# Cross-attention kernel: two more probability tiles turned off TensorE, PSUM shared by halves, normalization on ScalarE

## The chip, the cores and the metric

One core of one Trainium2 chip. The metric is the device time of one execution in microseconds, median of several runs. Before the change it is 120.97 us (three runs: 120.93, 120.97, 122.6).

## What is computed

The reference, cut to the arithmetic; x is (2, 512, 512), the memory (2, 1024, 256), all float32:

```python
memory_proj = jnp.einsum('bme,de->bmd', memory, W_mem)
scores = jnp.einsum('bnd,bmd->bnm', hidden_states, memory_proj) / jnp.sqrt(jnp.float32(D))
attn = jax.nn.softmax(scores, axis=-1)
memory_context = jnp.einsum('bnm,bmd->bnd', attn, memory_proj)
gate_input = jnp.concatenate([hidden_states, memory_context], axis=-1)
gate = jax.nn.sigmoid(jnp.einsum('bnf,df->bnd', gate_input, W_gate) + b_gate)
fused = hidden_states + gate * memory_context
return _rmsnorm(fused, norm_w)
```

## The kernel before

The kernel never forms the projected memory. It projects the queries through W_mem (`queries`), multiplies them with the memory's first form, `ctxT` (`scores`), takes a softmax, multiplies the probabilities with the memory's second form, `ctxN` (`attended`), and uses W_mem and the gate weights behind that (`gate_weights`, `gate_from_x`, `gate_from_attended`, `context`). There are two batches of four tiles of 128 rows: tiles j = 0 to 3 and j = 4 to 7.

Each float32 operand is split in a high and a low part, and each product is three matmuls: high-high, high-low, low-high. ScalarE makes the high part of a loaded block (`split_hi`, L344), VectorE the low part by subtraction (`split_lo`, L472), GpSimd for blocks from 28 on (L318). Loads go by SyncE in the order of `blocks` into a ring of 10 slots; load i waits until block i - 10 is split both ways. So the order of `blocks` is the order in which operands come.

A tile's way through softmax: `scores(j)` on TensorE into a pair of PSUM banks, `row_max` on VectorE (L482), `exponentials` on ScalarE (L358), `normalize` on VectorE (L489) in `probs`, which has three slots. Then `attended` needs the probabilities with memory positions on the partitions. Tiles 0 to 3 are turned by TensorE against an identity (`turn`, 8 transposes a tile, L730) into a PSUM pair, and split from there (L371 high, L512 low). Tiles 4 to 7 are turned without TensorE: VectorE transposes 32x32 blocks (`square_up`, L500) into ring slots, SyncE writes them to DRAM (`send`, L267, 512 KB) and reads them back in another block order (`fetch`, L278, 4 DMAs of 128 KB), and ScalarE and VectorE split them (`placed_hi` L366, `placed_lo` L506). `attended(b)` waits for all four tiles of its batch: the high parts at its start, the low parts before the last third.

PSUM holds `wide`, three pairs of banks, and `acc`, one pair. A list `uses` gives each use of a pair of `wide` the pair of its place modulo 3; a use waits for the release of the use three before it. A `gate` use takes a whole pair: one bank for the gate's sums, one for `context`.

The order on each engine is written out by hand, and every engine executes in order. `banks`, `wait_banks`, the `blocks` list, the SyncE program and the written-out orders are what the change touches.

Of the kernel before, what the change touches and what calls it, by code (L numbers as in the profile page):

```python
# [5 lines left out]
def xattn_kernel(nc, xT, ctxT, ctxN, w_mem, w_memT, w_gateT, x_rows, b_gate, norm_w, out):  # L6
    f32 = mybir.dt.float32
# [5 lines left out]
    P = 128  # L13
# [15 lines left out]
    with ctx:  # L29
# [24 lines left out]


        QUAD = 32
        NQ = P // QUAD
        squares_of = [ring[:, 2 * n:2 * n + 2].rearrange("p a n -> p (a n)") for n in range(2)]
        placed = [ring[:, 2 * n:2 * n + 2].rearrange("p a n -> p (a n)") for n in range(2, 4)]
        passage = [nc.dram_tensor(f"passage{t}", [P, M], f32).ap() for t in range(T)]  # L60
# [5 lines left out]
        bias = sb("bias", [P, D])  # L66
        gain = sb("gain", [P, D])
# [4 lines left out]
        res = sb("res", [P, 2, D])  # L72
        neg_max = sb("neg_max", [P, B * T])
# [57 lines left out]
        for k in range(KD):  # L131
            wgT_block(k)
# [37 lines left out]
        landed = [sem(f"landed{n}") for n in range(2)]  # L170
        q_hi, q_lo = sem("q_hi"), sem("q_lo")
# [16 lines left out]
        def nth_chunk(b, c):  # L188
# [3 lines left out]
        uses = [("scores", 0), ("scores", 1), ("scores", 2), ("turn", 0), ("scores", 3), ("turn", 1),  # L192
                ("turn", 2), ("wc", 0), ("turn", 3)]
        uses += [("scores", 4), ("scores", 5), ("scores", 6), ("gate", 0), ("scores", 7)]
        uses += [("gate", j) for j in range(1, B * T)]

        def banks(kind, j):
            return uses.index((kind, j)) % PAIRS

        def wait_banks(eng, kind, j):  # L200
            n = uses.index((kind, j)) - PAIRS
            if n < 0:
                return
            kind, i = uses[n]
            if kind == "scores":
                eng.wait_ge(exped, i + 1)
            elif kind == "turn":
                eng.wait_ge(pT_lo, i + 1)
            elif kind == "wc":
                eng.wait_ge(wc_lo, KE)  # L210
            else:
                eng.wait_ge(gated, i + 1)
# [22 lines left out]
        def from_quarters(t):  # L235
            return placed[t % 2].rearrange("p (q k n) -> p q k n", q=NQ, k=KM)
# [4 lines left out]
        def _(sp):  # L241
            def load_x(j):
                sp.dma_start(xr[:, j % 2], x_rows[j]).then_inc(x_loaded[j % 2], 16)

            for i, (src, _, _, key) in enumerate(blocks):
                if i in BY_ACT:
                    continue
                if i >= RING:
                    wait_hi(sp, i - RING)
                    wait_lo(sp, i - RING)  # L250
                sp.dma_start(slot(i), src).then_inc(loaded[i], 16)
                if key == ("ctxT", 1, KE - 1, 1):
                    sp.dma_start(bias[:], b_gate.partition_broadcast(P)).then_inc(vec_loaded, 16)
                    sp.dma_start(gain[:], norm_w.partition_broadcast(P)).then_inc(vec_loaded, 16)
                    load_x(0)
                    load_x(1)
# [8 lines left out]
            def send(t):  # L265
                sp.wait_ge(squared_up, t + 1)
                sp.dma_start(passage[t], squares_of[t % 2]).then_inc(sent[t % 2], 16)  # L267

            def fetch(t):

                if t < 2:
                    wait_lo(sp, NB - 1)
                else:
                    sp.wait_ge(pT_lo, T + t - 1)
                sp.wait_ge(sent[t % 2], 16 * (t // 2 + 1))
                quarters = passage[t].rearrange("(q j) (r f) -> r j q f", q=NQ, r=NQ)
                for r in range(NQ):
                    sp.dma_start(placed[t % 2][r * QUAD:(r + 1) * QUAD].rearrange("j (q f) -> j q f", q=NQ),  # L278
                                 quarters[r]).then_inc(landed[t % 2], 16)

            send(0)
            fetch(0)
            send(1)
            fetch(1)
            send(2)
            next_x(2)
            fetch(2)
            store(0)
            send(3)
            fetch(3)  # L290
            next_x(3)
            store(1)
# [40 lines left out]
        def _(act):  # L333
# [18 lines left out]
            def exponentials(j):  # L352
                act.wait_ge(maxed, j + 1)
                if j - PROBS >= T:
                    act.wait_ge(squared_up, j - PROBS - T + 1)
                elif j >= PROBS:
                    act.wait_ge(turned, j - PROBS + 1)
                nc.scalar.activation(probs[:, j % PROBS].rearrange("p (h m) -> p h m", h=2),  # L358
                                     wide[:, banks("scores", j)], ACT.Exp, bias=neg_max[:, j:j + 1],
                                     accum_out=row_sum[:, j:j + 1]).then_inc(exped, 1)  # L360

            def placed_hi(t):
                act.wait_ge(landed[t % 2], 16 * NQ * (t // 2 + 1))
                if t == 0:
                    act.wait_ge(a_sum, nth_chunk(0, KE - 1))
                nc.scalar.activation(by_quarter(pT_s[0], t), from_quarters(t), ACT.Copy).then_inc(pT_hi, 1)  # L366

            def turned_hi(j):
                act.wait_ge(turned, j + 1)
                rows = slice(j % T * P, (j % T + 1) * P)  # L370
                nc.scalar.activation(pT_s[0][:, :, rows],  # L371
                                     wide[:, banks("turn", j)].rearrange("p h (k n) -> p (h k) n", n=P),
                                     ACT.Copy).then_inc(pT_hi, 1)

            def weight_hi(c):
                act.wait_ge(wc_sum, c + 1)
                nc.scalar.activation(wcT_s[0][:, c], wide[:, banks("wc", 0), c], ACT.Copy).then_inc(wc_hi, 1)
# [12 lines left out]
            def mean_square(j):  # L390
                act.wait_ge(fused, j + 1)
                if j == 0:
                    act.wait_ge(eps_set, 1)
                nc.scalar.activation(squares[:], gate[:, j % 2], ACT.Square, scale=SCALE,  # L394
# [6 lines left out]
            split_hi(11, 12, 13)  # L401
            exponentials(0)
            split_hi(14, 15)
            exponentials(1)
            split_hi(16)
            exponentials(2)
            turned_hi(0)
            split_hi(17, 18)
            turned_hi(1)
            exponentials(3)  # L410
            query_hi(1, 0)
            split_hi(19)
            query_hi(1, 1)
            turned_hi(2)
            split_hi(20, 21)
            weight_hi(0)
            turned_hi(3)
            split_hi(22, 23)
            weight_hi(1)
            split_hi(*range(24, 34))  # L420
# [3 lines left out]
            exponentials(4)  # L424
            exponentials(5)
            exponentials(6)
            gate_tanh(0)
            placed_hi(0)
            mean_square(0)
            exponentials(7)  # L430
            placed_hi(1)
            gate_tanh(1)
            placed_hi(2)
            mean_square(1)
            gate_tanh(2)
            placed_hi(3)
            mean_square(2)
            gate_tanh(3)
# [23 lines left out]
        def _(dve):  # L462
# [17 lines left out]
            def row_max(j):  # L480
                dve.wait_ge(scores_sum, j + 1)
                nc.vector.reduce_max(neg_max[:, j:j + 1], wide[:, banks("scores", j)], AXIS.XY,  # L482
                                     negate=True).then_inc(maxed, 1)
# [405 lines left out]
```

## Time and profile before

| | |
|---|---|
| median of three runs | 120.97 us |
| the profiled execution | 120.74 us |
| its span | 119.0 us |
| mean granted TensorE clock | 0.987 of full |
| ScalarE busy | 55.1 us (46%) |
| VectorE busy | 76.7 us (64%) |
| GpSimd busy | 19.5 us (16%) |
| the chain that ended last | 85% of the span on TensorE |

The span is the stretch of the execution in which instructions run; the rest of its 120.74 us, 1.7 us, lies around it. The page lists each engine's busy time, the span in 40 slices, the chain followed back from the last instruction, and the costliest groups of instructions. The timeline gives an instruction's start, its duration and, in brackets, how long its engine was idle ahead of it and what ended that. Matmuls overlap, so a matmul's duration is longer than the step from one start to the next.

### The profile page before, as it was taken

The page shows a single profiled execution, that of the slowest core. Times are in us where ns is not written, and L with a number is a line of the kernel's source. Part 1 is how long each engine was busy: PE and PEld are TensorE (multiplying, and loading weights), DVE is VectorE, ACT ScalarE, POOL GpSimd, SP SyncE. Part 2 cuts the span into 40 slices and gives each one's busy share as a digit, 9 for nine tenths or more (in the row PEclk, how much of TensorE's full clock was granted, in tenths as well). Part 3 has the DMA queues.
Part 4 walks back from the last instruction along what each step waited for, and adds up shares of the span by engine and source line. Part 5 has one row for each costly group of instructions (what it writes and reads, how often), then busy time and mean ns, then how long its engine had stood idle before and what let it go on. Part 6 is the DMA issues. An engine that isn't in the chain of part 4 may idle for free.

```text
span 119.0 us, 1570 instructions
## 1 busy us (share of the span) xinstructions
PE 112.3 (94%) x547; PEld 94.2 (79%) x547; DVE 76.7 (64%) x116; ACT 55.1 (46%) x100; POOL 19.5 (16%) x25
## 2 busy tenths in 40 slices
PE   6999999999999999999999999999999999999910
PEld 6878888888888888888888888888888888889900
DVE  0389969987999700459999857464662031777791
ACT  4498675559967930941624532512421030334511
POOL 2000000000000499692000300030301000011120
PEclk9999999999999999999999999999999999999995
DMA  3999992436955870000436495749222200044222
GB/s 54 338 343 357 390 389 77 150 111 187 265 198 167 248 258 10 0 0 0 176 116 237 116 323 158 293 116 241 83 88 102 80 0 0 0 123 141 88 88 88
DMA packets 11095, 18.45 MB, mean 155 GB/s; under 512 B 1232, under 2 KB 4048, under 8 KB 11088
## 3 DMA queue, kind: packets, MB, share of 16 engines
q1 hardware_dynamic: 10656, 17.70, 45.2%
q10 hardware_dynamic: 432, 0.66, 1.8%
q8 instruction: 4, 0.07, 0.2%
q14 instruction: 3, 0.02, 0.1%
HBM read 14.16 MB, written 4.19 MB: 154 GB/s over the span
## 4 chain that ended last, share of the span: by engine, by line
PE 85%; issue 4%; DVE 4%; ACT 2%; POOL 1%; POOLq 1%; DVEq 0%; ACTq 0%
PE wide L716 18%; PE acc L767 18%; PE wide L785 16%; PE acc L691 10%; PE wide L813 6%; PE wide L798 6%; PE wide L744 5%; PE wide L676 3%; PE wide L730 3%; ACT squares L394 2%; DVE gate L546 2%; DVE gate L539 2%; POOL rstd L323 1%; POOLq L29 1%; ACT res L457 0%
## 5 line engine op out<-in xcount | busy, mean ns | idle before, releaser
L323 POOL TENSOR_TENSOR rstd<-mean_sq,neg_half 128x1 f32<-128x1 f32 x8 | 5.9, 734 | 55.7 <-ACT squares L394 52.6
L358 ACT ACTIVATE probs<-wide,neg_max 128x1024 f32<-128x1024 f32 x8 | 8.9, 1116 | 8.4 <-DVE neg_max L482 8.4
L716 PE MATMUL wide<-ctxT_hi,qT_hi 128*128 128x512 f32 x32 | 12.6, 392 | 0.0
L716 PE MATMUL wide<-ctxT_hi,qT_lo 128*128 128x512 f32 x32 | 12.5, 389 | 0.0
L716 PE MATMUL wide<-ctxT_lo,qT_hi 128*128 128x512 f32 x32 | 12.5, 389 | 0.0
L318 POOL TENSOR_TENSOR wgT_lo<-ring,wgT_hi 128x512 fp32r<-128x512 f32 x4 | 5.4, 1373 | 38.9 <-ACT wgT_hi L344 38.9
L523 DVE TENSOR_TENSOR wgT_lo<-acc,wgT_hi 128x512 fp32r<-128x512 f32 x4 | 2.6, 686 | 13.6 <-ACT wgT_hi L383 13.6
L482 DVE TENSOR_REDUCE neg_max<-wide 128x1 f32<-128x1024 f32 x8 | 9.7, 1215 | 2.2 <-PE wide L716 2.1
L387 ACT ACTIVATE gate<-gate 128x512 f32<-128x512 f32 x7 | 4.4, 629 | 13.2 <-DVE gate L533 13.2
L785 PE MATMUL wide<-wgT_hi,xT_lo 128*128 128x512 f32 (+1 forms) x36 | 8.8, 365 | 0.0
L785 PE MATMUL wide<-wgT_lo,xT_hi 128*128 128x512 f32 (+1 forms) x36 | 8.8, 365 | 0.0
L785 PE MATMUL wide<-wgT_hi,xT_hi 128*128 128x512 f32 (+1 forms) x36 | 8.8, 365 | 0.0
L366 ACT ACTIVATE pT_hi<-ring 128x1024 fp32r<-128x1024 f32 x4 | 4.2, 1062 | 9.1 <-DMA ring<-passage 9.1
L506 DVE TENSOR_TENSOR pT_lo<-ring,pT_hi 128x1024 fp32r<-128x1024 f32 x4 | 4.9, 1222 | 5.0 <-ACT pT_hi L366 5.0
L394 ACT ACTIVATE squares<-gate 128x513 f32<-128x513 f32 x7 | 4.4, 628 | 7.5 <-DVE gate L546 7.5
L554 DVE SCALAR_TENSOR_TENSOR res<-gate,rstd,gain 128x512 f32<-128x512 f32 x7 | 5.2, 745 | 3.9 <-POOL rstd L323 3.9
L767 PE MATMUL acc<-pT_lo,ctxN_hi 128*128 128x512 f32 x32 | 7.6, 389 | 0.0
L767 PE MATMUL acc<-pT_hi,ctxN_hi 128*128 128x512 f32 x32 | 7.6, 389 | 0.0
L767 PE MATMUL acc<-pT_hi,ctxN_lo 128*128 128x512 f32 x32 | 7.6, 389 | 0.0
L383 ACT ACTIVATE wgT_hi<-acc 128x512 fp32r<-128x512 f32 x4 | 2.2, 596 | 11.7 <-PE acc L767 11.7
L785 PEld LDWEIGHTS wide<-wgT_hi,xT_hi 128*128 128x128 f32 x36 | 6.4, 188 | 1.2
L785 PEld LDWEIGHTS wide<-wgT_hi,xT_lo 128*128 128x128 f32 x36 | 6.4, 189 | 1.1
(91 smaller groups left out, 250.9 us busy)
## 6 DMA issues: line engine op xcount, KB each, us to landing
ring<-ctxT SPq DMA_DIRECT2D x8, 256.0 KB, 4.1
ring<-w_gateT SPq DMA_DIRECT2D x8, 256.0 KB, 5.5
ring<-ctxN SPq DMA_DIRECT2D x8, 256.0 KB, 5.4
xr<-x_rows SPq DMA_DIRECT2D x8, 256.0 KB, 3.3
passage<-ring SPq DMA_DIRECT2D x4, 512.0 KB, 3.6
ring<-passage SPq DMA_DIRECT2D x16, 128.0 KB, 2.8
out<-res SPq DMA_DIRECT2D x7, 256.0 KB, 2.0
ring<-xT SPq DMA_DIRECT2D x6, 256.0 KB, 5.5
```

The lines of the kernel that those rows point to most:

```text
L318: nc.gpsimd.tensor_tensor(lo, slot(i), hi.bitcast(f32), ALU.subtract).then_inc(lo_pool, 1)
L323: nc.gpsimd.tensor_tensor(rstd[:, col], mean_sq[:, col], neg_half[:], ALU.pow)\
L358: nc.scalar.activation(probs[:, j % PROBS].rearrange("p (h m) -> p h m", h=2), wide[:, banks("scores", j)], ACT.Exp, bias=neg_max[:, j:j + 1],
L394: nc.scalar.activation(squares[:], gate[:, j % 2], ACT.Square, scale=SCALE, accum_out=mean_sq[:, j:j + 1]).then_inc(squared, 1)
L482: nc.vector.reduce_max(neg_max[:, j:j + 1], wide[:, banks("scores", j)], AXIS.XY, negate=True).then_inc(maxed, 1)
L691: last = nc.tensor.matmul(acc[:, c], wm_s[left][:, c, k], xT_s[right][:, b, k], start=(k == 0 and (left, right) == (HI, HI)), stop=(k == K ...
L716: last = nc.tensor.matmul(wide[:, banks("scores", j), h], qT_s[left][:, c, rows], ctxT_s[right][:, c, cols], start=(c == 0 and (left, righ ...
L744: last = nc.tensor.matmul(wide[:, banks("wc", 0), c], wm_s[left][:, c, k], wgT_s[right][:, KD + k], start=(k == 0 and (left, right) == (HI ...
L767: last = nc.tensor.matmul(acc[:, c], ctxN_s[left][:, k, c * P:(c + 1) * P], pT_s[right][:, k], start=(k == 0 and (left, right) == (HI, HI) ...
L785: nc.tensor.matmul(wide[:, banks("gate", j), h, cols], xT_s[left][:, b, k, rows], wgT_s[right][:, k, cols], start=(k == 0 and (left, right ...
L798: last = nc.tensor.matmul(wide[:, banks("gate", j), h, cols], aT_s[left][:, c, rows], wcT_s[right][:, c, cols], start=False, stop=(left == ...
L813: last = nc.tensor.matmul(sums, aT_s[left][:, c, rows], wmT_s[right][:, c, cols], start=(c == 0 and (left, right) == (HI, HI)), stop=(left ...
```

## The change

1. Tiles 0 and 1 no longer go through `turn`. They take the way of tiles 4 to 7: block transpose on VectorE, `send`, `fetch`, split. Their squares lie in a new buffer `spare` and in `res`, their placed form in `xr` and in `vecs` (which holds bias and gain). The loads of x rows, bias and gain therefore wait for the low splits of tiles 0 and 1.
2. `normalize` moves from VectorE to ScalarE, as a copy with a scale; VectorE keeps the reciprocal (`invert`).
3. `uses` now names its pair and halves itself. Gate and context sums are uses of their own, of one half each; a gate half is free once `gate_arg` has read it.
4. The four blocks of gate weights for x (blocks 28 to 31 before) come as blocks 20 to 23, ahead of `ctxN` (now 24 to 27) and `ctxT` of the second batch (now 28 to 31, so that GpSimd makes its low halves).
5. The orders change. TensorE runs `scores(3)` ahead of the second batch's queries, `gate_from_x(0)` and `(1)` ahead of `attended(0)`, and spreads `context` behind later tiles.

```diff
+        EARLY = 2
+        BY_DMA = (*range(EARLY), *range(T, B * T))
+        squares_of = {0: spare[:], 1: res[:].rearrange("p a n -> p (a n)")}
+        placed = {0: xr[:].rearrange("p a n -> p (a n)"), 1: vecs[:].rearrange("p a n -> p (a n)")}
...
         for k in range(KD, 2 * KD):
             wgT_block(k)
+        for k in range(KD):
+            wgT_block(k)
         for j in range(KM // 2):
             ctxN_block(0, j)
...
-        for k in range(KD):
-            wgT_block(k)
...
+        BOTH = (0, 1)
+        uses = [("scores", 0, 0, BOTH), ("scores", 1, 1, BOTH), ("scores", 2, 2, BOTH), ("scores", 3, 0, BOTH),
...
+                ("context", 2, 0, (0,)), ("context", 3, 0, (1,)), ("gate", 5, 2, (1,)), ("gate", 6, 1, (0,)),
...
+            n = use_of[kind, j]
+            for half in uses[n][3]:
+                before = [u for u in uses[:n] if u[2] == uses[n][2] and half in u[3]]
+                if not before:
+                    continue
+                of, i = before[-1][0:2]
...
+                elif of == "gate":
+                    eng.wait_ge(arg_done, i + 1)
+                else:
+                    eng.wait_ge(gated, i + 1)
...
+            load(*range(27))
             send(0)
+            load(27, 28)
             fetch(0)
             send(1)
+            load(29, 30, 31, 32)
             fetch(1)
+            load(33, 34, 35, 36)
+            load_x(0)
+            load_x(1)
+            load_vecs()
+            load(37)
+            send(T)
+            send(T + 1)
+            fetch(T)
+            fetch(T + 1)
+            send(T + 2)
+            send(T + 3)
             next_x(2)
...
+            def normalize(j):
+                act.wait_ge(inv_done, j + 1)
+                nc.scalar.activation(probs[:, j % PROBS], probs[:, j % PROBS], ACT.Copy,
+                                     scale=inv_sum[:, j:j + 1]).then_inc(normed, 1)
...
-            def normalize(j):
+            def invert(j):
                 dve.wait_ge(exped, j + 1)
                 nc.vector.reciprocal(inv_sum[:, j:j + 1], row_sum[:, j:j + 1]).then_inc(inv_done, 1)
-                dve.wait_ge(inv_done, j + 1)
-                nc.vector.tensor_scalar(probs[:, j % PROBS], probs[:, j % PROBS], inv_sum[:, j:j + 1], None,
-                                        ALU.mult).then_inc(normed, 1)
...
+                if b == 0:
+                    pe.wait_ge(early_hi, EARLY)
+                pe.wait_ge(pT_hi, nth_tile(b, T - 1) - EARLY)
```

TensorE between the third turned tile and `attended(0)`, in the kernel before (L730 is `turn`, L744 `gate_weights`, L767 `attended`):

```order
L730 MATMUL wide<-ident,probs 128x128 x8
L744 MATMUL wide<-wgT_hi,wm_hi 128x512 x4
L744 MATMUL wide<-wgT_lo,wm_hi 128x512 x4
L744 MATMUL wide<-wgT_hi,wm_lo 128x512 x4
L767 MATMUL acc<-pT_hi,ctxN_hi 128x512 x16
```

and in the changed one (L809 is `turn`, L823 `gate_weights`, L868 `gate_from_x`, L850 `attended`):

```order
L809 MATMUL wide<-ident,probs 128x128 x8
L823 MATMUL wide<-wgT_hi,wm_hi 128x512 x4
L823 MATMUL wide<-wgT_lo,wm_hi 128x512 x4
L823 MATMUL wide<-wgT_hi,wm_lo 128x512 x4
L868 MATMUL wide<-wgT_hi,xT_hi 128x512 x4
L868 MATMUL wide<-wgT_lo,xT_hi 128x512 x4
L868 MATMUL wide<-wgT_hi,xT_lo 128x512 x4
L868 MATMUL wide<-wgT_hi,xT_hi 128x512 x4
L868 MATMUL wide<-wgT_lo,xT_hi 128x512 x4
L868 MATMUL wide<-wgT_hi,xT_lo 128x512 x4
L850 MATMUL acc<-pT_hi,ctxN_hi 128x512 x16
```

The last turn before `attended(0)` and its gate weights are as they were; 24 matmuls of `gate_from_x` now follow them.

ScalarE from the last splits of the second batch's queries input to the second batch's `query_hi`, before (L344 `split_hi`, L358 `exponentials`, L371 the high split of a turned tile, L350 `query_hi`):

```order
L358 ACTIVATE probs,row_sum<-wide,neg_max 128x1024
L344 ACTIVATE xT_hi<-ring 128x512 x2
L358 ACTIVATE probs,row_sum<-wide,neg_max 128x1024
L344 ACTIVATE wgT_hi<-ring 128x512
L358 ACTIVATE probs,row_sum<-wide,neg_max 128x1024
L371 ACTIVATE pT_hi<-wide 128x8x128
```

and after (L400 `split_hi`, L414 `exponentials`, L420 `normalize`):

```order
L400 ACTIVATE wgT_hi<-ring 128x512
L414 ACTIVATE probs,row_sum<-wide,neg_max 128x1024
L400 ACTIVATE wgT_hi<-ring 128x512 x2
L420 ACTIVATE probs<-probs,inv_sum 128x1024
L400 ACTIVATE wgT_hi<-ring 128x512 x2
L414 ACTIVATE probs,row_sum<-wide,neg_max 128x1024
L400 ACTIVATE wgT_hi<-ring 128x512
L420 ACTIVATE probs<-probs,inv_sum 128x1024
L414 ACTIVATE probs,row_sum<-wide,neg_max 128x1024
L400 ACTIVATE wgT_hi<-ring 128x512
L420 ACTIVATE probs<-probs,inv_sum 128x1024
```

Three normalizations stand between the exponentials, and the splits ahead of the first exponential have grown by three.

SyncE after the gate weights' loads, in the changed kernel (L282 loads, L305 `send`, L322 `fetch`; `ring` is the target of the loads, `spare` and `res` the squares of tiles 0 and 1, `xr` and `vecs` their placed form):

```order
L282 DMA ring<-ctxN 128x512 x3
L305 DMA passage<-spare 128x1024
L282 DMA ring<-ctxN 128x512
L282 DMA ring<-ctxT 128x512
L322 DMA xr<-passage 32x4x256 x4
L305 DMA passage<-res 128x1024
L282 DMA ring<-ctxT 128x512 x3
L282 DMA ring<-w_memT 128x512
L322 DMA vecs<-passage 32x4x256 x4
```

Before, this stretch held loads only; now two sends and two fetches of four DMAs each stand in the same queue, with loads behind each of their waits.

## Rows read from the trace of the kernel before

**Rows 1.** The page, parts 1 and 2: TensorE's busy time and its granted clock

```profile
PE 112.3 (94%) x547; PEld 94.2 (79%) x547; DVE 76.7 (64%) x116; ACT 55.1 (46%) x100; POOL 19.5 (16%) x25
...
PEclk9999999999999999999999999999999999999995
```

**Rows 2.** Waits: engine, line <- whom: total us, times, longest; then a weight load

```profile
PE wide L676 <- DVE warm L463: 1.0, 1, 1.0
...
PEld wide L744 <- DVE wgT_lo L472: 0.2, 1, 0.2
```

**Rows 3.** The chain that ended last, in order of time: start us, us, what

```profile
19.69 2.73 PE acc L691 x12
22.42 0.87 PE wide L730 x8
23.29 2.77 PE wide L716 x12
...
26.93 2.74 PE acc L691 x12
...
30.55 2.84 PE wide L744 x12
...
34.26 2.74 PE wide L744 x12
37.00 10.88 PE acc L767 x48
...
85.95 10.88 PE acc L767 x48
```

**Rows 4.** ScalarE's timeline: start us, us, line, operation, out<-in, idle before

```profile
15.55 1.12 ACT L358 ACTIVATE probs<-wide,neg_max 128x1024 f32<-128x1024 f32 x1 [1.82 <-DVE neg_max L482]
...
16.65 1.14 ACT L344 ACTIVATE xT_hi<-ring 128x512 fp32r<-128x512 f32 x2
...
37.53 2.18 ACT L344 ACTIVATE ctxT_hi<-ring 128x512 fp32r<-128x512 f32 x4
...
64.17 1.06 ACT L366 ACTIVATE pT_hi<-ring 128x1024 fp32r<-128x1024 f32 x1 [1.58 <-DMA ring<-passage]
...
82.84 1.07 ACT L366 ACTIVATE pT_hi<-ring 128x1024 fp32r<-128x1024 f32 x1 [2.34 <-DMA ring<-passage]
...
116.10 0.51 ACT L457 ACTIVATE res<-res,rstd 128x256 f32<-128x256 f32 x1 [1.55 <-POOL rstd L323]
```

**Rows 5.** VectorE's timeline, same columns

```profile
18.34 0.75 DVE L489 TENSOR_SCALAR probs<-probs,inv_sum 128x1024 f32<-128x1024 f32 x1
...
38.30 2.48 DVE L472 TENSOR_TENSOR ctxT_lo<-ring,ctxT_hi 128x512 fp32r<-128x512 f32 x4
...
50.63 1.23 DVE L482 TENSOR_REDUCE neg_max<-wide 128x1 f32<-128x1024 f32 x1 [1.03 <-PE wide L716]
...
56.01 1.23 DVE L500 STREAM_TRANSPOSE ring<-probs 128x1024 f32<-128x1024 f32 x1
```

**Rows 6.** SyncE's timeline, its DMA issues: a send and two fetches

```profile
57.27 0.33 SPq L267 DMA_DIRECT2D passage<-ring  x1
59.94 1.75 SPq L278 DMA_DIRECT2D ring<-passage  x4
...
77.47 1.74 SPq L278 DMA_DIRECT2D ring<-passage  x4
```

**Rows 7.** The page, DMA issues: count, KB each, us from issue to landing

```profile
ring<-w_gateT SPq DMA_DIRECT2D x8, 256.0 KB, 5.5
...
xr<-x_rows SPq DMA_DIRECT2D x8, 256.0 KB, 3.3
passage<-ring SPq DMA_DIRECT2D x4, 512.0 KB, 3.6
```

**Rows 8.** GpSimd's timeline: four splits

```profile
40.31 5.38 POOL L318 TENSOR_TENSOR wgT_lo<-ring,wgT_hi 128x512 fp32r<-128x512 f32 x4 [38.93 <-ACT wgT_hi L344]
```

**Rows 9.** Line 730, the turns' matmuls: ns min/median/max, first and last start

```profile
L730 PE MATMUL wide<-ident,probs x32: 270/272/273, 22.3 to 34.0; 128*128 128x128 f32 x32
```

More of the change, by code:

```diff
@@ L65, in xattn_kernel @@
         table = sb("table", [P, 1])
-        bias = sb("bias", [P, D])
-        gain = sb("gain", [P, D])
+        vecs = sb("vecs", [P, 2, D])
+        bias, gain = vecs[:, 0], vecs[:, 1]
+        spare = sb("spare", [P, M])
         xr = sb("xr", [P, 2, D])
@@ L241, in _, with load, load_vecs @@
         def _(sp):
+            def load(*ids):
+                for i in ids:
+                    if i in BY_ACT:
+                        continue
+                    if i >= RING:
+                        wait_hi(sp, i - RING)
+                        wait_lo(sp, i - RING)
+                    sp.dma_start(slot(i), blocks[i][0]).then_inc(loaded[i], 16)
             def load_x(j):
+                if j < 2:
+                    sp.wait_ge(early_lo, 1)
                 sp.dma_start(xr[:, j % 2], x_rows[j]).then_inc(x_loaded[j % 2], 16)
[L245 to L256, printed above, removed]
+            def load_vecs():
+                sp.wait_ge(early_lo, EARLY)
+                sp.dma_start(bias, b_gate.partition_broadcast(P)).then_inc(vec_loaded, 16)
+                sp.dma_start(gain, norm_w.partition_broadcast(P)).then_inc(vec_loaded, 16)
             def next_x(j):
@@ L715, in scores @@
                                     pe.wait_ge(q_lo, nth_chunk(b, c))
-                            last = nc.tensor.matmul(wide[:, banks("scores", j), h], qT_s[left][:, c, rows],
+                            last = nc.tensor.matmul(sums("scores", j, h), qT_s[left][:, c, rows],
                                                     ctxT_s[right][:, c, cols],
@@ L797, in gate_from_attended @@
                         for c in range(KE):
-                            last = nc.tensor.matmul(wide[:, banks("gate", j), h, cols], aT_s[left][:, c, rows],
+                            last = nc.tensor.matmul(sums("gate", j, h)[:, cols], aT_s[left][:, c, rows],
                                                     wcT_s[right][:, c, cols], start=False,
@@ L812, in context @@
                                 wait_lo(pe, index_of["wmT", c])
-                            last = nc.tensor.matmul(sums, aT_s[left][:, c, rows],
+                            last = nc.tensor.matmul(made, aT_s[left][:, c, rows],
                                                     wmT_s[right][:, c, cols],
@@ L825, in _ @@
                 queries(0, c, range(KD // 2, KD))
-            scores(0)
-            scores(1)
-            scores(2)
-            queries(1, 0, range(KD))
-            turn(0)
-            scores(3)
-            turn(1)
-            queries(1, 1, range(KD))
+            for j in range(T):
+                scores(j)
+            for c in range(KE):
+                queries(1, c, range(KD))
             turn(2)
@@ L837, in _ @@
             gate_weights(1)
+            gate_from_x(0)
+            gate_from_x(1)
             attended(0)
@@ L840, in _ @@
             scores(5)
-            for t in range(T):
-                if t < 2:
-                    scores(6 + t)
-                gate_from_x(t)
-                gate_from_attended(t)
-                context(t)
-            gate_from_x(T)
-            gate_from_x(T + 1)
+            gate_from_attended(0)
+            scores(6)
+            gate_from_attended(1)
+            scores(7)
+            context(0)
+            context(1)
+            for j in (2, 3):
+                gate_from_x(j)
+                gate_from_attended(j)
+            gate_from_x(4)
+            context(2)
+            context(3)
+            gate_from_x(5)
             attended(1)
-            gate_from_x(T + 2)
+            gate_from_x(6)
             for j in range(T, LAST):
```

301 lines of the change are left out of this document (169 added, 132 removed).

## The prediction

> **What bounds the kernel now.** I read the page first. TensorE (PE) is busy 94% of the span at nearly full granted clock [rows 1]. Busy time alone proves little for a pipelined engine, so I went to the waits: PE waited once, 1.0 us for its warm-up operand, and its weight loads once for 0.2 us in the gate-weight product [rows 2]. The chain that ended last says the same: from the first matmul to the last tiles it is one PE piece after another, with no issue time between them [rows 3]. So PE's instruction stream is the kernel, and the rest need only be in time. What PE no longer does is gained whole, unless something new is late. A step of 12 matmuls takes 10.88 / 4 = 2.72 us [rows 3]; all PE times below are chain times.
>
> **What leaves PE.** turn(0) and turn(1), 8 transposes each. From 22.42 to the end of the piece at 26.93 + 2.74 = 29.67 lie both turns and two 12-matmul steps: 7.25 - 2 x 2.72 = 1.81 us for two turns, with the slower restart behind each (2.77 and 2.74 instead of 2.72) [rows 3]. The first gate-weight product took 2.84 where the second took 2.74 [rows 3]: that is PE's 0.2 us wait for a low half of the gate weights [rows 2], of which 0.10 shows in the chain. In the new order DVE has split these halves by 26.1, well ahead of the product at 28.7, so 0.10 goes too. No matmul is added. Sum on PE: -1.91 us.
>
> **What is new on the others, and whether it is in time.** Durations: a split on ScalarE (ACT) advances it 0.52 us, (2.18 for four, less 0.1 of overlap with the next), an exponential with its accumulator read 1.10 (15.55 to 16.65), a 1024-column copy 1.06, or 0.97 after overlap [rows 4]. On VectorE (DVE) a row maximum is 1.23, a 32x32-block transpose 1.23, a split 0.60, and the normalization that goes away 0.75 [rows 5]. Normalizing on ACT is not in the trace. Lower bound: the 0.75 of DVE; upper bound: four times the 256-column scaled copy of the last tile, 4 x 0.51 = 2.04 [rows 4, 5]. I take 1.06, since the 1024-column copy is the same engine, size and function.
>
> PE now runs scores 0 to 3 from 11.53 to 22.41, the second batch's queries to 27.85, turn(2) to 28.7, gate weights, turn(3) at 31.46, gate weights, two gate_from_x from 35.07, attended(0) from 40.51 (before: 37.00).
>
> First batch on ACT: splits 14 to 16 fit ahead of the first exponential, which still starts at 15.55 behind row maximum 0. Then 2 splits, normalize(0) 17.7 to 18.8, 2 splits, exponential 1 from 19.7, a split, normalize(1) 21.8 (held by DVE's reciprocal behind its transpose), exponential 2 from 22.8, a split, normalize(2) 24.4 to 25.5, queries, exponential 3 from 25.9, normalize(3) 28.4 to 29.4. PE asks for tile 2 at 27.85 (2.3 us spare), tile 3 at 31.46 (2.0 spare), and the pair of scores(0) at 19.69, free since 16.75. At 2.04 each, three normalizations put tile 2 at 28.5 and four put tile 3 at about 33.4: PE would wait some 0.6, then 1.3 more; the change then gives nothing but 0.0 to 0.1 us. The cover is those 2 us.
>
> First transport, tiles 0 and 1: DVE turns blocks of tile 0 in 19.4 to 20.6 and of tile 1 in 24.4 to 25.6. Load 26 on SyncE (SP) needs the low half of block 16, made at 19.4, so it is out by 19.9 and the send goes at 20.7. Behind its wait stand loads 27 and 28, whose ring slots come free only at 22.5 and 24.3 anyway. A send takes 3.6 us [rows 7], and the first fetch row followed its send by 2.67 [rows 6]; so fetch(0) at 24.7 to 26.5, send(1) 26.5, loads 29 to 32 until 29.3, fetch(1) at 30.2. From a fetch's first issue to the high copy took 64.17 - 59.94 = 4.2 us in the best case and 82.84 - 77.47 = 5.4 in the worst [rows 4, 6]. So tile 1 lands at 34.4 to 35.6; ACT reaches it at 35.7, behind the second gate-weight copy, and is done at 36.8. PE wants it at 40.51: 3.7 us spare. The low half (DVE, by 38.1) is wanted two thirds through attended(0), at 47.8. The memory's second form (loads 24 to 27) is split by 37.2; GpSimd now makes the low half of the next batch's first form, at 1.35 us each from 37.8 on [rows 8], done by 43.2 and wanted at 51.4. So what hides the two tiles is the 5.44 us of gate_from_x put ahead of attended(0): without it tile 1 would be 1.7 us late.
>
> Second batch: row maximum 4 ends 1.4 us after scores(4), at 55.5, exponential 4 at 56.7; scores(6), which takes over its pair, starts at 58.2, 1.5 spare. Scores(7) wants exponential 5 (59.3) at 62.3. Of the shared halves the nearest is context(3), at 79.9 behind gate_arg(3), which DVE finishes at 77.7. The last tile's transport: blocks turned by 70.3 (before 69.2), send at once, fetch(7) behind fetch(6) and an x load at 76.2 instead of 77.47 [rows 6]; with the 5.4 us of the same tile before, the copy ends at 82.7. Attended(1) starts at 85.95 - 1.91 = 84.04 [rows 3], 1.3 spare, against 85.95 - 83.91 = 2.0 before [rows 3, 4]. The tail behind attended(1) has the same work and moves as a whole.
>
> **A rule against the row.** Rows first: the profile gives a transpose 272 ns [rows 9], while 8 of them take 0.87 us of the chain [rows 3], 109 ns each, since they overlap. The Trainium skill ("TensorE: Matmul & The Clock Gate", Part 4) has about 275 ns for a transpose in a kernel's context, "It's the only path that does a full 128×128 transpose in one shot". By it two turns would cost 16 x 0.275 = 4.4 us, an estimate. The trace agrees with the duration but not with the cost.
>
> [...]
>
> **Sum.** The profiled execution took 120.74 us, of which the span is 119.0. 120.74 - 1.91 = 118.83, span 117.1. The shown median, 120.97, is 0.23 above it, so as a median 118.8 to 119.1: I say 119.0, which is 1.6% less. A change within 2%, 118.55 to 123.4, is about what a measurement of this kernel can tell from none.
>
> **Rivals.** (A, forecast) PE stays gapless: 118.3 to 119.6. Chance 0.76.
>
> (B) Partly given back. Either ACT's normalizations are near 2.04 (up to 1.9 us of PE waiting, worked out above), or tile 7 is late by more than its 1.3 us at attended(1). For it: ACT and DVE now wait on each other in turn (reciprocal, normalize, block transpose), and SP's in-order queue passes each delay on. Against: a delay of 3.2 us is needed before everything is lost. 119.6 to 121.1, chance 0.11.
>
> (C) Slower: the first transport under load. Its transfers run beside the block loads. A 256 KB load took 5.5 us where the queue was full, 3.3 where it was not [rows 7]: a factor of 1.67. Then send(0) lands at 26.7, fetch(0) ends at 28.5, send(1) lands at 34.5, and fetch(1), at 5.4 x 1.67 = 9.0, at 43.5. The copy ends at 44.6, PE waits 4.1 us in front of attended(0), and the time is 122.9. It decides from 3.7 us of delay, and passes the old time from 5.6. Against it: the loads then queued are one by one, gated by ring slots, not a burst. Chance 0.08, of which 0.05 over 123.4 with knock-on delays.
>
> (D) Faster by far: the turns cost what their durations say, 16 x 0.272 = 4.35 us [rows 9], and the time is 120.97 - 4.45 = 116.5. Against it, the 0.87 us pieces. Chance 0.03. The remaining 0.02 I give to a gain that I don't see.
>
> **How the numbers follow.** Faster by over 2%: D, the unseen gain, and the lowest part of A (below 118.55, about 0.05): 0.10. Slower: 0.05. Within 2%: 0.85. The range for 8 in 10 starts at A's low end, 118.3, and takes in the upper bound of the normalization, 121.1. A's own range is 118.3 to 119.6.
>
> **What would show it.** Right: 16 transposes instead of 32; PE's waits still only the warm-up; attended(0) starting near 40.4 and attended(1) near 84.0; a span near 117.1. ACT's scaled copy near 1.06 us; turn(2) preceded by no idle time. Wrong: a PE wait for the copy out of vecs (C), for a turn's normalized tile, or for the copy out of the ring at attended(1) (B); or a span under 116.5 without waits (D). If normalize takes over 1.7 us, my ACT schedule fails; if the two fetches take over 9 us in all from send(1), my transport does.

## The result and the profile after

The changed kernel takes 119.06 us (median of six runs, 118.69 to 119.44) against 120.97 us before. The ratio is 0.985, 95% interval 0.983 to 0.988: 1.5% faster, and short of the 2% that count as more than no change. The profiled execution took 119.02 us with a span of 117.3. The ratios leave slow executions out, and the profiled ones of four versions below (normalization back on VectorE, the table's "both" and "all from 27 on behind", and the third tile) are slow: their scores start at 13.3 to 13.5 us instead of 11.3 to 11.9, so only distances within them are compared.

The page of the changed kernel, answering to [rows 1], with the busy share of the DMA engines:

```profile
PE 109.9 (94%) x531; PEld 91.6 (78%) x531; DVE 72.6 (62%) x110; ACT 63.7 (54%) x108; POOL 18.7 (16%) x25
...
PEclk9999999999999999999999999999999999999998
DMA  3999996879999947000040979898215000044222
```

TensorE's share is still 94%, 16 of its instructions and 2.4 us of its overlapping busy time are gone, and the clock is granted throughout. VectorE lost 4.1 us and ScalarE gained 8.6. The chain that ended last, answering to [rows 3] (start us, us, what; L795 is `scores`, L770 the queries, the other lines as above; an `issue` piece, further below, is time in which TensorE stands idle):

```profile
11.47 10.88 PE wide L795 x48
22.35 5.44 PE acc L770 x24
27.79 0.87 PE wide L809 x8
28.67 2.75 PE wide L823 x12
...
32.28 2.76 PE wide L823 x12
35.05 5.44 PE wide L868 x24
40.49 11.05 PE acc L850 x48
...
84.17 10.88 PE acc L850 x48
```

Attended(1) starts 1.78 us earlier than before (84.17, 85.95 in [rows 3]). Term by term: the stretch that held the two turns took 7.26 us before (22.42 to 29.68 in [rows 3]) and is now two steps of 2.72, so 1.82 us are gone. The gate-weight products take 2.75 and 2.76 instead of 2.84 and 2.74, 0.07 less. The first scores start 0.06 earlier. And one piece is longer: attended(0) has 11.05 us from 40.49 to 51.53 where it had 10.88, a loss of 0.17. 1.82 + 0.07 + 0.06 - 0.17 = 1.78, and the last piece, ScalarE's at 114.32 against 116.10 in [rows 4], has moved by the same 1.78.

So the sum on TensorE held. What didn't hold is how much time the others had. ScalarE's timeline of the changed kernel (start us, us, what, idle before): the third and fourth normalization, then the copies of tiles 1 and 7.

```profile
24.59 1.14 ACT L420 ACTIVATE probs<-probs,inv_sum 128x1024 f32<-128x1024 f32 x1
...
28.32 1.14 ACT L420 ACTIVATE probs<-probs,inv_sum 128x1024 f32<-128x1024 f32 x1
...
39.25 1.06 ACT L431 ACTIVATE pT_hi<-vecs 128x1024 fp32r<-128x1024 f32 x1 [3.56 <-DMA vecs<-passage]
...
82.28 1.06 ACT L431 ACTIVATE pT_hi<-ring 128x1024 fp32r<-128x1024 f32 x1 [2.92 <-DMA ring<-passage]
```

A normalization on ScalarE takes 1.14 us, and tiles 2 and 3 are normalized at 25.7 and 29.5, as forecast. But the copy of tile 1 ends at 40.31 instead of 36.8. The waits of TensorE (PE) and of its weight loads (PEld), total us, times, longest:

```profile
PE acc L770 <- ACT xT_hi L400: 0.8, 1, 0.8
...
PEld acc L850 <- issue: 0.3, 1, 0.3
```

The first lies ahead of the scores, which start no later for it. The second is the weight load for attended(0): it was idle for 0.32 us up to 40.38, so it could have started 0.25 us before the copy's end. The 3.7 us of forecast slack were all gone, and this wait shows as the 0.17 us that attended(0) takes longer. SyncE's issues show where they went:

```profile
25.32 1.75 SPq L322 DMA_DIRECT2D xr<-passage  x4
27.11 0.43 SPq L305 DMA_DIRECT2D passage<-res  x1
...
32.17 1.75 SPq L322 DMA_DIRECT2D vecs<-passage  x4
...
76.25 1.89 SPq L322 DMA_DIRECT2D ring<-passage  x4
```

The send at 27.11 is followed by its fetch only at 32.17, 5.1 us later, and 7.1 us pass from there to the copy at 39.25. The forecast had 3.7 and 5.4. The windows say why (length, TensorE busy, granted clock, DMA share, GB/s): the changed kernel,

```profile
26.00:32.00 6.00, 6.00 (x35) 1.00 1.01 261
32.00:40.00 8.00, 8.00 (x38) 1.00 1.06 292
```

and the kernel before around its first transports in the second batch:

```profile
61.00:65.00 4.00, 4.00 (x20) 1.00 0.76 261
65.00:70.00 5.00, 5.00 (x24) 1.00 0.56 182
```

A share near 1 (fourth figure) means that all 16 DMA engines are busy, and so they are from 26 to 40 us in the changed kernel. Before, in these two windows, a quarter (0.76) and over two fifths (0.56) of their time was free.

### The profile page after: what moved, and what is told of

Same layout as the page of the kernel before. It is cut to its first block, busy times and chain, and to the rows that moved or that the text cites. A ratio compares the mean times of both kernels' runs of the same rounds, so it can differ in the third digit from the quotient of the medians.

```text
span 117.3 us, 1564 instructions
## 1 busy us (share of the span) xinstructions
PE 109.9 (94%) x531; PEld 91.6 (78%) x531; DVE 72.6 (62%) x110; ACT 63.7 (54%) x108; POOL 18.7 (16%) x25
## 4 chain that ended last, share of the span: by engine, by line
PE 81%; issue 4%; DVE 4%; ACT 3%; DMA 3%; POOL 1%; POOLq 1%; DVEq 0%; ACTq 0%
PE acc L850 19%; PE wide L795 19%; PE wide L868 16%; PE acc L770 10%; PE wide L898 6%; PE wide L881 6%; PE wide L823 5%; DMA ring<-w_mem 3%; ACT squares L462 2%; DVE gate L624 2%; DVE gate L617 2%; PE wide L809 1%; POOL rstd L379 1%; POOLq L29 1%; ACT xT_hi L400 0%
## 5 line engine op out<-in xcount | busy, mean ns | idle before, releaser
L379 POOL TENSOR_TENSOR rstd<-mean_sq,neg_half 128x1 f32<-128x1 f32 x8 | 4.9, 617 | 51.2 <-ACT squares L462 48.1
L795 PE MATMUL wide<-ctxT_hi,qT_hi 128*128 128x512 f32 x32 | 12.4, 389 | 0.0
L795 PE MATMUL wide<-ctxT_lo,qT_hi 128*128 128x512 f32 x32 | 12.4, 389 | 0.0
L795 PE MATMUL wide<-ctxT_hi,qT_lo 128*128 128x512 f32 x32 | 12.4, 389 | 0.0
L374 POOL TENSOR_TENSOR ctxT_lo<-ring,ctxT_hi 128x512 fp32r<-128x512 f32 x4 | 5.5, 1400 | 40.0 <-ACT ctxT_hi L400 40.0
L414 ACT ACTIVATE probs<-wide,neg_max 128x1024 f32<-128x1024 f32 x8 | 8.9, 1110 | 2.5 <-DVE neg_max L558 2.4
L420 ACT ACTIVATE probs<-probs,inv_sum 128x1024 f32<-128x1024 f32 x8 | 9.2, 1144 | 0.6 <-DVE inv_sum L563 0.5
L868 PE MATMUL wide<-wgT_lo,xT_hi 128*128 128x512 f32 (+1 forms) x36 | 8.8, 365 | 0.0
L868 PE MATMUL wide<-wgT_hi,xT_lo 128*128 128x512 f32 (+1 forms) x36 | 8.8, 365 | 0.0
L868 PE MATMUL wide<-wgT_hi,xT_hi 128*128 128x512 f32 (+1 forms) x36 | 8.8, 365 | 0.0
L850 PE MATMUL acc<-pT_hi,ctxN_hi 128*128 128x512 f32 x32 | 7.7, 392 | 0.0
L850 PE MATMUL acc<-pT_hi,ctxN_lo 128*128 128x512 f32 x32 | 7.6, 389 | 0.0
L850 PE MATMUL acc<-pT_lo,ctxN_hi 128*128 128x512 f32 x32 | 7.6, 389 | 0.0
L868 PEld LDWEIGHTS wide<-wgT_hi,xT_hi 128*128 128x128 f32 x36 | 6.4, 188 | 1.2
L632 DVE SCALAR_TENSOR_TENSOR res<-gate,rstd,vecs 128x512 f32<-128x512 f32 x7 | 5.2, 749 | 3.2 <-POOL rstd L379 3.2
L868 PEld LDWEIGHTS wide<-wgT_hi,xT_lo 128*128 128x128 f32 x36 | 6.4, 189 | 1.1
```

Of the source, the lines that this page charges most:

```text
L379: nc.gpsimd.tensor_tensor(rstd[:, col], mean_sq[:, col], neg_half[:], ALU.pow)\
L420: nc.scalar.activation(probs[:, j % PROBS], probs[:, j % PROBS], ACT.Copy, scale=inv_sum[:, j:j + 1]).then_inc(normed, 1)
L795: last = nc.tensor.matmul(sums("scores", j, h), qT_s[left][:, c, rows], ctxT_s[right][:, c, cols], start=(c == 0 and (left, right) == (HI, ...
L850: last = nc.tensor.matmul(acc[:, c], ctxN_s[left][:, k, c * P:(c + 1) * P], pT_s[right][:, k], start=(k == 0 and (left, right) == (HI, HI) ...
L868: nc.tensor.matmul(sums("gate", j, h)[:, cols], xT_s[left][:, b, k, rows], wgT_s[right][:, k, cols], start=(k == 0 and (left, right) == (H ...
```

## The experiments

**What a turn costs.** The kernel before, with the transposes of tiles 0 and 1 done twice:

```diff
-                for k in range(KM):
+                for k in [*range(KM)] * (2 if j < 2 else 1):
```

> The kernel before, with the 8 transposes of tiles 0 and 1 issued twice each on TensorE, into the same place, and nothing else changed. It prices a turn by itself. The theory (a turn costs its 0.87 us piece of the chain, 109 ns a transpose in the middle of a row of them): the second 8 join the first, so 16 more transposes cost 16 x about 0.10 to 0.11 = 1.6 to 1.8 us, and the time is 122.6 to 122.8. Rival D (a transpose costs the 272 ns that its row says): 16 x 0.272 = 4.35 us more, 125.3. Waits elsewhere should stay as they are, since every tile of the first batch comes up to 1.8 us later and everything behind it moves with TensorE.

Measured: 123.05 us, ratio to before 1.022 (1.015 to 1.030). Its chain of waits:

```profile
22.41 1.75 PE wide L730 x16
...
26.90 1.75 PE wide L730 x16
...
38.74 10.88 PE acc L767 x48
...
85.08 3.01 PE wide L785 x12
```

16 transposes take 1.75 us where 8 take 0.87: 109 ns each, as the theory had it, and not 272. By attended(0) the kernel is 1.74 us late (38.74 against 37.00). Another 0.3 us appears in the piece at 85.08, a product of 2.72 us that took 3.01 in front of attended(1), where the weight loads waited 0.5 us for VectorE to read a PSUM bank; the run lies above the forecast of 122.6 to 122.8 by about that much. Part 4 of the Trainium skill's "TensorE: Matmul & The Clock Gate", about 275 ns for a transpose, gives the duration of one row here, not what it takes of TensorE's time.

**Only the turns.** The changed kernel with tiles 0 and 1 turned by TensorE again, their sends and fetches gone, all else kept (the main lines):

```diff
-        EARLY = 2
+        EARLY = 0
...
             for c in range(KE):
+                turn(c)
                 queries(1, c, range(KD))
```

> The changed kernel with one part undone: tiles 0 and 1 are turned by TensorE again (one turn ahead of each of the second batch's two query products), their sends and fetches are gone, and the x rows, bias and gain load without waiting. Normalization on ScalarE, the shared halves, the block order and TensorE's new order stay. The theory (the two turns leaving TensorE are the whole gain): 1.8 us slower than the changed kernel, less the 0.17 us that attended(0) loses there, so 120.6 to 121.0, level with the kernel before. Rival (the halves, the order or the normalization on ScalarE are worth something by themselves): clearly under 120.3.

Measured: 120.89 us, ratio 1.001 (0.998 to 1.003). Together, the shared halves, the new orders and ScalarE's normalization bring nothing as long as the turns stay; the gain is the two turns. What each of these parts does alone no run shows; the next one takes the normalization back with the turns gone.

**Normalization back on VectorE.** The changed kernel with `tensor_scalar` on VectorE behind each reciprocal, and none on ScalarE:

```diff
             def invert(j):
...
+                dve.wait_ge(inv_done, j + 1)
+                nc.vector.tensor_scalar(probs[:, j % PROBS], probs[:, j % PROBS], inv_sum[:, j:j + 1], None,
+                                        ALU.mult).then_inc(normed, 1)
```

> The changed kernel with one part undone: the normalization is back on VectorE, right behind each reciprocal; ScalarE has only the exponentials, splits and tanh. The theory (TensorE never waited for a normalized tile, ScalarE had 2 us to spare): no change from the changed kernel beyond 0.3 us, 118.8 to 119.4; the first send starts at much the same time. Rival (the normalization on ScalarE was needed for the early transport to be in time): the wait in front of attended(0) grows beyond 1 us, 120 or more.

Measured: 121.99 us, ratio to before 1.011 (1.007 to 1.014). My theory fell; the rival holds. Its chain (L786 is `scores`, L841 `attended`):

```profile
13.34 10.88 PE wide L786 x48
...
42.36 1.54 issue
43.89 11.13 PE acc L841 x48
...
87.66 0.95 issue
88.61 11.16 PE acc L841 x48
```

TensorE waits 1.54 us in front of attended(0) and 0.95 in front of attended(1), and both products take about 0.26 longer than 10.88: 3.0 us in all. This execution started its scores 1.87 us later than the changed kernel's (13.34, 11.47), so distances from there are what can be compared. The block transpose of tile 1 on VectorE starts 14.8 us behind the first scores instead of 12.8, since three normalizations, which advance it by some 0.67 us each, stand ahead of it, and the copy of tile 1 starts 29.4 us behind them instead of 27.8. In the second batch the last block transpose starts 30.3 us behind the start of attended(0) instead of 28.6.

**The cover.** The changed kernel with the two gate_from_x behind attended(0):

```diff
-            gate_from_x(0)
-            gate_from_x(1)
             attended(0)
+            gate_from_x(0)
+            gate_from_x(1)
```

> The changed kernel with gate_from_x(0) and (1) put behind attended(0) instead of ahead of it; the same matmuls in all. The theory (these 5.44 us are what hides the transport of tiles 0 and 1, whose copy ended at 40.3 in the changed kernel's trace): attended(0) would start at 35.05 and waits until the copy, about 5.2 us, so 124.0 to 124.5. By the working of the prediction (copy done at 36.8) it would wait 1.7 us, 120.8. If the transport speeds up or slows down with TensorE's order, the copy's time moves; I expect it to stay within 1 us of 39.3.

Measured: ratio 1.047 (1.040 to 1.054), 125.98 us over all runs, more than the 124.0 to 124.5 expected, and 124.3 in the profiled one. Its chain and its windows:

```profile
34.91 3.68 issue
38.59 12.74 PE acc L850 x48
```

```profile
38.00:39.00 1.00, 0.41 (x2) 1.00 0.98 326
39.00:42.00 3.00, 3.00 (x9) 0.53 0.89 294
42.00:43.00 1.00, 1.00 (x4) 0.69 0.94 188
43.00:47.00 4.00, 4.00 (x19) 1.00 0.38 106
```

The wait is 3.68 us, not 5.2, as the copy came at 37.4. But attended(0) then takes 12.74 instead of 10.88: behind the idle stretch the granted clock (third figure) is 0.53 from 39 to 42 us and 0.69 to 43, so mostly at the lower of its two levels, 1.2 GHz instead of 2.4, and the product takes 1.86 more. The other three executions had a mean granted clock of 0.968 to 0.970 where the profiled one had 0.980, and took 1.0 to 2.6 us more; they have no trace, so how long their clock was low isn't shown. The prediction had "without it tile 1 would be 1.7 us late", a third of the 5.5 us found.

**What stretches the transport.** Five versions move or hold the loads around tile 1's send and fetch. SyncE's order in the changed kernel is send(1), loads 29 to 32, fetch(1), loads 33 to 36. The first holds back only what comes behind:

```diff
             fetch(1)
+            sp.wait_ge(early_landed[1], 16 * NQ)
             load(33, 34, 35, 36)
```

> The changed kernel, but SyncE waits until fetch(1) has landed before it issues loads 33 to 36, the x rows, bias and gain. In the changed kernel's trace the DMA engines are busy all through 28 to 40 us, and tile 1's copy starts 7.1 us after fetch(1)'s first issue where the second batch took 4.2 to 5.4. Theory K (the loads queued behind the fetch share its engines and stretch it): the copy out of vecs starts 1.5 to 2.5 us earlier, at 36.8 to 37.8, attended(0)'s piece shrinks from 11.05 to 10.88, and the time is 118.8 to 119.1. Rival L (only what is queued ahead matters, since each engine works its queue in order): the copy stays at 38.8 to 39.4.

The second moves what is ahead:

```diff
-            load(29, 30, 31, 32)
             fetch(1)
+            load(29, 30, 31, 32)
             load(33, 34, 35, 36)
```

> The changed kernel with fetch(1) issued ahead of loads 29 to 32 instead of behind them; these four loads go out right after it. The theory (TensorE had only 0.1 us to spare at attended(0), and loads queued ahead stretch both the send and the fetch): the send is alone, so fetch(1) goes out at 30.5 to 31.0 instead of 32.2, and the copy starts at 35.5 to 37.5; attended(0) starts unhindered, 10.88 instead of 11.05; the time is 118.8 to 119.0, 0.1 to 0.2 below the changed kernel. Rival (what is queued behind counts as much as what is ahead): the copy stays within 1 us of 39.3 and the time at 119.06.

The third does both (the wait and the move):

> The changed kernel with fetch(1) ahead of loads 29 to 32 and with SyncE waiting until it has landed before any further load. The transport of tile 1 then shares the DMA engines with nothing but what was issued before its send. The theory (contention is the whole difference between the 12.1 us from send to copy here and the 8.5 us of the second batch): 8.0 to 9.0 us from the send's issue to the copy, copy starting at 35.1 to 36.1, behind the second gate-weight copy. Rival (the early transport is slower for another reason, such as its target or SyncE's issue): still 10 us or more. The loads come 3 to 4 us later than in the changed kernel; GpSimd's low halves are done by about 48 against 51.4 wanted, so the time stays at 118.8 to 119.1.

The fourth moves loads 27 and 28 too:

```diff
             send(0)
-            load(27, 28)
             fetch(0)
             send(1)
-            load(29, 30, 31, 32)
             fetch(1)
+            load(27, 28)
+            load(29, 30, 31, 32)
             load(33, 34, 35, 36)
```

> The changed kernel with both early sends and fetches ahead of every load from 27 on: send(0), fetch(0), send(1), fetch(1), then loads 27 to 36. With fetch(1) ahead of loads 29 to 32 alone, the send of tile 1 still took 5.3 us until its fetch went out, where the second batch took 3.7. Theory M (loads 27 and 28, 512 KB issued 2.5 to 4 us ahead of the send, are still on the DMA engines): send(1) goes out at 25.7, fetch(1) at 29.4 to 30.0, the copy would start by 34.5 and ends by 36.8 behind the gate-weight copy. Rival N (the send of the first batch is slower for another reason): still 5 us or more from send(1) to fetch(1). Load 27 comes at about 31.5 and is wanted at 43.2 in attended(0), so TensorE has no wait either way and the time is 118.7 to 119.0, like the version with only loads 29 to 32 behind.

and the fifth is that with `gate_from_x(1)` behind attended(0):

> The version with all loads from 27 on behind fetch(1), and gate_from_x(1) behind attended(0), so that only 2.72 us of work stand ahead of it and it would start at 37.6 to 37.8. If the copy of tile 1 ends by 36.8, TensorE doesn't wait and the time stays at 118.7 to 119.1: half of the cover was needed only because the transport was stretched. If the copy still ends at 38.5 or later (rival N), there is a wait of 1 us or more, 119.8 to 121.

Start times from SyncE's and ScalarE's timelines of each profiled execution, us; the time is the median, the ratio is to the kernel before:

| | send(1) | fetch(1) | copy of tile 1 | send to fetch | fetch to copy | time, ratio |
|---|---|---|---|---|---|---|
| changed kernel | 27.11 | 32.17 | 39.25 | 5.06 | 7.08 | 119.06, 0.985 (0.983 to 0.988) |
| loads behind held | 27.42 | 32.51 | 38.07 | 5.09 | 5.56 | 119.11, 0.983 (0.981 to 0.986) |
| loads 29 to 32 behind | 26.71 | 32.04 | 36.39 | 5.33 | 4.35 | 118.89, 0.982 (0.979 to 0.984) |
| both | 28.54 | 34.02 | 38.39 | 5.48 | 4.37 | 118.95, 0.982 (0.979 to 0.985) |
| all from 27 on behind | 28.46 | 32.07 | 37.38 | 3.61 | under 5.31 | 119.18, 0.984 (0.981 to 0.987) |
| the same, half the cover | 26.64 | 30.30 | 35.42 | 3.66 | under 5.12 | 119.12, 0.985 (0.980 to 0.989) |

In the last two the copy didn't wait for the DMA, only for ScalarE to come to it, so it had landed earlier (rows of the last):

```profile
34.93 0.60 ACT L443 ACTIVATE wm_hi<-wide 128x512 fp32r<-128x512 f32 x1 [0.21 <-PE wide L823]
35.42 1.05 ACT L431 ACTIVATE pT_hi<-vecs 128x1024 fp32r<-128x1024 f32 x1
```

Theory M holds, N falls: with loads 27 and 28 gone from in front of it, the send takes the 3.6 us of [rows 7] again, where no other version moved its 5.1 to 5.5. Loads 29 to 32 ahead of the fetch cost 2.7 us of fetch to copy (7.08 to 4.35). With these gone, loads behind cost nothing (4.35 and 4.37); with these still ahead, holding back the ones behind brought 1.5 (7.08 to 5.56), so neither K nor L is the whole of it, and why the loads behind count in one order and not in the other isn't shown. With both changes 9.85 us still pass from send to copy, where 8.0 to 9.0 were expected of contention alone. I had expected the send to profit from moving loads 29 to 32: it didn't, which is what pointed to loads 27 and 28. All five run without a wait of TensorE behind its start, and their times don't differ beyond their intervals; with nearly 4 us regained (the copy at 35.42 instead of 39.25), half the cover is enough.

**Both together.** VectorE's normalization with loads 29 to 32 behind the fetch:

> Normalization back on VectorE (which took 121.99 by itself, with 1.8 us of waiting and slow restart in front of attended(0) and 1.2 in front of attended(1)), and fetch(1) ahead of loads 29 to 32. If the normalization on ScalarE matters only because the two transports have so little to spare, the earlier fetch takes the wait at attended(0) away and leaves the one at attended(1): 119.9 to 120.7. If something else of VectorE's load costs it, it stays at 121.5 to 122.3.

Measured: 120.82 us, ratio 0.996 (0.992 to 0.999); ratio times the 121.03 of before gives 120.5. Its chain (L800 is `turn`):

```profile
27.74 1.05 PE wide L800 x8
...
31.54 1.04 PE wide L800 x8
...
40.77 10.88 PE acc L841 x48
...
84.28 0.65 issue
84.93 11.12 PE acc L841 x48
```

The wait at attended(0) is gone, the one at attended(1) has stayed. The two turns that are left take 1.05 and 1.04 us instead of 0.87, as their weight loads waited (0.7 us in all). So ScalarE's normalization earns its place at both transports, and in this version 0.35 us at the turns as well. These pieces account for the 120.04 us of the profiled execution; the runs lie between 119.45 and 122.31, and what spreads them isn't shown.

**A third tile.** On the version with all loads behind, tile 2 also goes through DRAM, its squares in `spare` again and its placed form in `gate`:

```diff
-        EARLY = 2
+        EARLY = 3
...
+        squares_of[2], placed[2] = spare[:], gate[:].rearrange("p a n -> p (a n)")[:, 0:M]
...
             send(1)
+            send(2)
             fetch(1)
+            fetch(2)
...
-            turn(2)
             gate_weights(0)
```

> Tile 2 taken off TensorE as well: its squares go through spare again (free once send(0) is done), its placed form lies in gate, whose constant column is set afterwards; SyncE runs send(0), fetch(0), send(1), send(2), fetch(1), fetch(2), then loads 27 on. TensorE has one turn left. The theory (a turn is worth 0.87 to 0.93 us as long as its copy is there before attended(0)): attended(0) would start at 39.5; send(2) goes out at about 27.3, the three transports share the DMA engines, fetch(2) follows at 33 and its copy should end at 38 to 39.3. Then the time is 117.9 to 118.2, 1.0 below the changed kernel. Rival (the DMA engines are full between 27 and 38 us, and 1 MB more stretches the last fetch past 39.5): a wait in front of attended(0) of 1 us or more gives the turn's price back, 118.9 to 120.

Measured: 119.97 us (six executions, 118.24 to 121.17), ratio 0.985 (0.980 to 0.991): nothing over the changed kernel. The time is the rival's and not the theory's 117.9 to 118.2, but the rival's wait in front of attended(0) isn't there. Its chain (L859 is `attended`), and ScalarE's copies of tiles 2 and 7:

```profile
41.65 10.88 PE acc L859 x48
...
85.17 0.85 issue
86.02 11.15 PE acc L859 x48
```

```profile
39.38 1.06 ACT L434 ACTIVATE pT_hi<-gate 128x1024 fp32r<-128x1024 f32 x1 [1.57 <-DMA gate<-passage]
...
84.86 1.06 ACT L434 ACTIVATE pT_hi<-ring 128x1024 fp32r<-128x1024 f32 x1 [2.92 <-DMA ring<-passage]
```

Attended(0) was in time and starts 28.1 us behind the scores (at 13.52 in this execution), where the changed kernel has 29.0: the turn's 0.9 us were gained there. 1.1 us were given back at attended(1): TensorE comes there earlier, tile 7's transport doesn't. I had worked out only the first transport. The last run moves tile 7's fetch ahead of a store and a load:

```diff
             fetch(T + 2)
+            fetch(T + 3)
             store(0)
             next_x(3)
-            fetch(T + 3)
```

> The version with three tiles off TensorE, and the second batch's last fetch ahead of the store of tile 0 and the x load in SyncE's order. In the version before it attended(0) was in time (41.65, copy done at 40.44) and the wait had moved to attended(1): 0.85 us, and a piece of 11.15 instead of 10.88, 1.1 in all, since tile 7's copy ended at 85.92. The theory (each of the two attended products has its own transport in front of it, and at the second it is SyncE's two issues, 1.0 us, that now count): fetch(7) goes out at 1.8 us behind fetch(6) instead of 2.8, the copy of tile 7 ends 0.9 us earlier, the wait shrinks to 0.3 or less, and the time is 118.0 to 118.5. Rival (the copy waits for shared DMA engines, not for SyncE's issue): the wait stays at 0.6 or more and the time at 118.9 to 119.4.

Measured: 118.43 us, ratio 0.981 (0.975 to 0.988), span 116.7.

```profile
39.88 11.16 PE acc L859 x48
...
83.68 10.88 PE acc L859 x48
```

```profile
38.72 1.06 ACT L434 ACTIVATE pT_hi<-gate 128x1024 fp32r<-128x1024 f32 x1 [2.09 <-DMA gate<-passage]
...
80.58 1.06 ACT L434 ACTIVATE pT_hi<-ring 128x1024 fp32r<-128x1024 f32 x1 [0.39 <-DMA ring<-passage]
```

Tile 7's copy now ends at 81.64, 2.0 us ahead of attended(1); the wait is gone. Attended(0) has 11.16 us, with tile 2's copy ending 0.1 us ahead of it. This version is faster than the kernel before. Against the changed kernel its median is 0.6 us lower, but the intervals of the two ratios overlap, so that isn't settled.

## Why the prediction was right

The forecast was 119.0 us in 118.3 to 121.1, case A with no wait of TensorE; measured 119.06. That the two agree to 0.06 us is in part chance: on TensorE 1.78 us went, not 1.91, and the medians of so few runs move by some tenths.

- **What bounds it:** held. With TensorE's stream as the bound, two turns added cost their price by attended(0), and two turns removed were the whole gain.
- **The price of the turns:** 1.81 forecast, 1.82 measured. Case D fell with 109 ns a transpose.
- **The 0.10 us of gate weights:** 0.07. The sum left out 0.06 us gained ahead of the scores and 0.17 us lost in attended(0).
- **ScalarE's and VectorE's schedule, apart from the transports:** within 0.4 us. Normalize(2) ran 24.6 to 25.7 (forecast 24.4 to 25.5), normalize(3) ended at 29.5 (29.4), exponential 4 at 56.7 (56.7); a normalization took 1.14, where I took 1.06.
- **The first transport:** wrong by 3.5 us, and it came out at 119.06 only because 3.7 us of slack had been there; that it sufficed is luck, not working. The recorded sign against this step, over 9 us from send(1) to the end of its fetch, was met. The step that failed is "A send takes 3.6 us", with the 3.7 us to the fetch that I made of it, together with the 4.2 to 5.4 us for the fetch. These are rows from a stretch with DMA engines partly free, and I argued in case C that the loads were gated one by one and thus no burst. Their sum still fills the engines: a share of 1.01 to 1.06. The mechanism of C was there, at 12.1 us from send to copy against its 15.0 and the forecast's 7.9 to 9.1 (C stretched both legs by 1.67; the send took 1.4 times its 3.6 us, the fetch 1.3 times its 5.4). What it cost was 0.17 us in attended(0), which is back at 10.88 in each version whose copy came a microsecond or more earlier.
- **The cover:** the forecast 1.7 us of lateness without it were 3.7 us of waiting and 1.9 more in attended(0), most of it from the lower clock.
- **ScalarE's normalization:** I priced it as a risk alone. I didn't ask what VectorE's queue gains by it, and so missed that undoing it costs 3 us: tile 1's block transpose on VectorE then starts 2 us later and tile 7's 1.7, and neither transport has the slack for it.
- **The second transport:** fetch(7) at 76.25 (forecast 76.2), the copy done at 83.34 (82.7), 0.8 us ahead of attended(1) (1.3).

## What to carry to other kernels

Where one engine's stream is the bound, price what leaves it by its share of the chain, not by its instructions' durations, and then spend the effort on the slack of everything that has to be ready for it. A DRAM round trip taken from a quieter stretch of the trace is a lower bound: read the DMA share of the stretch where it will run, and count every byte ahead of each leg, including loads issued three to five microseconds earlier. When the bound moves up by a microsecond, each later deadline moves up too; the gain lasts only to the next one without slack.

## What the runs showed of the hardware

- An idle stretch of 3.68 us on TensorE was followed, from about half a microsecond into the next product, by some three and a half microseconds at a granted clock of mostly 0.5 (1.2 GHz), and that product took 1.86 us more than 10.88. After idle stretches of 1.54, 0.95, 0.85 and 0.65 us it took only 0.24 to 0.28 us more, and the granted clock stayed at 1.00 behind each of them. From 0.17 to 0.28 us are also lost where TensorE is never idle but its weight loads wait 0.3 to 0.4 us for a late copy (11.05 in the changed kernel, 11.16 in the last run), so these quarter microseconds aren't a matter of the clock.
- DMAs already under way slow a later one on the same queue: 512 KB of loads issued 2.8 to 4.6 us ahead of a 512 KB send cost it 1.4 to 1.9 us. The Trainium skill ("Trainium Kernel Development and Optimization", Key Constraints) says that DMAs of all queues run on the same 16 engines and interleave; here all came from SyncE's queue, so no run shows that of other queues.
